# Decayed attention: projections and splits two heads earlier, q spread ahead of k, the division one score later

## The reference

```python
B, S, E, H = (2, 256, 128, 16)
D = E // H
b, s, e = x.shape
qkv = x @ Wqkv_w.T + Wqkv_b
qkv = qkv.reshape(b, s, 3, H, D).transpose(2, 0, 3, 1, 4)
q, k, v = (qkv[0], qkv[1], qkv[2])
scores = jnp.einsum('bhsd,bhtd->bhst', q, k) / jnp.sqrt(jnp.asarray(D, x.dtype))
dist = jnp.abs(idx[:, None] - idx[None, :])
decay = jnp.exp(-jnp.abs(distance_decay[0]) * dist)
scores = scores * decay
attn = jax.nn.softmax(scores, axis=-1)
out = jnp.einsum('bhst,bhtd->bhsd', attn, v)
out = out.transpose(0, 2, 1, 3).reshape(b, s, e)
return out @ out_w.T + out_b
```

## Time and profile before

| | |
|---|---|
| median of 3 runs | 2450.01 us (2449.64 to 2451.04) |
| the profiled execution | 2449.7 us, of which the traced span is 2447.9 us |
| busy share: PE, DVE, ACT, POOL | 90%, 67%, 61%, 69% |
| mean granted TensorE clock | 0.962 of full speed |
| phase `a` | some 1045 to 1701 us |

### The profile page before, as it was taken

The page is one execution under the profiler, slowest core; times in us unless marked ns, Lnnn a source line. Parts: engine busy times, 40 slices in busy tenths (PEclk is TensorE's granted clock), DMA queues, the critical chain, the costliest instruction groups (busy, mean ns, idle before and its releaser), DMA issues.

```text
span 2447.9 us, 60289 instructions
## 1 busy us (share of the span) xinstructions
PE 2202.7 (90%) x19744; PEld 1500.7 (61%) x19760; DVE 1628.1 (67%) x3905; ACT 1487.5 (61%) x4130; POOL 1679.2 (69%) x1712
## 2 busy tenths in 40 slices
PE   6998799998989998949998889998999979999989
PEld 4776467775657775525555555554677755677755
DVE  5777578875567775636665566666788755677755
ACT  3555378886378886325554455554788853788853
POOL 6777699884188884247665667665899831888842
PEclk8999899999999998979999999999999999999999
DMA  4000011121111111121101110110111211111111
GB/s 108 1 0 1 6 39 31 27 46 28 41 43 36 36 34 26 36 61 53 43 21 41 52 46 20 38 52 17 29 37 28 46 23 46 41 36 33 35 28 49
DMA packets 121250, 86.69 MB, mean 35 GB/s; under 512 B 85560, under 2 KB 102160, under 8 KB 118800
## 3 DMA queue, kind: packets, MB, share of 16 engines
q1 hardware_dynamic: 119248, 82.70, 14.1%
q10 hardware_dynamic: 1856, 2.23, 0.3%
HBM read 30.38 MB, written 8.39 MB: 16 GB/s over the span
## 4 chain that ended last, share of the span: by engine, by line
PE 50%; DVE 12%; POOL 9%; issue 8%; DMA 5%; SPq 3%; ACT 1%; DVEq 0%; POOLq 0%
PE bank L1170 8%; POOL store L1010 6%; PE bank L519 6%; PE bank L638 5%; PE bank L1161 4%; PE bank L1181 4%; DMA store<-parts 4%; PE bank L553 3%; PE bank L566 3%; PE bank L592 3%; PE bank L647 3%; PE bank L533 3%; DVE store L842 2%; POOL store L1019 2%; DVE store L847 2%
## 5 line engine op out<-in xcount | busy, mean ns | idle before, releaser
L1398 POOL TENSOR_SCALAR store<-store 128x512 f32<-128x512 f32 x512 | 349.8, 697 | 217.9 <-DVE store L1315 216.2
L1272 ACT ACTIVATE store<-bank 128x512 f32<-128x512 f32 x512 | 285.9, 604 | 316.4 <-PE bank L1170 315.6
L1315 DVE CUSTOM_DVE_ANT_0 store<-bank,store 128x512 f32<-128x512 f32 x512 | 340.2, 689 | 189.4 <-PE bank L1161 118.9
L730 ACT ACTIVATE store<-bank,store 128x128 f32<-128x128 f32 x1024 | 364.2, 378 | 68.6 <-DVE store L860 68.5
L1010 POOL TENSOR_TENSOR store<-store 128x16 f32<-128x16 f32 x128 | 372.6, 2911 | 26.4 <-DVE store L856 26.4
L1004 POOL TENSOR_TENSOR store<-store 128x512 f32<-128x512 f32 x256 | 321.2, 1276 | 83.3 <-DVE store L847 82.0
L1170 PEld LDWEIGHTS bank<-store 128*128 128x128 f32 x2048 | 252.4, 147 | 136.3 <-ACT store L1272 78.3
L1170 PE MATMUL bank<-store 128*128 128x128 f32 x2048 | 309.7, 285 | 0.0
L519 PE MATMUL bank<-store 128*128 128x512 f32 x512 | 268.8, 612 | 8.5 <-DVE store L835 7.0
L1019 POOL TENSOR_TENSOR store<-store 128x512 f32<-128x512 f32 x256 | 261.6, 1043 | 17.4 <-POOL store L1010 11.4
L1161 PE MATMUL bank<-store 72*128 72x512 bf16 x512 | 186.6, 397 | 86.1 <-DMA store<-parts 46.8
(11 more groups left out here) (199 smaller groups left out, 4457.7 us busy)
## 6 DMA issues: line engine op xcount, KB each, us to landing
store<-store SPq DMA_DIRECT2D x256, 128.0 KB, 2.3
store<-parts SPq DMA_DIRECT2D x96, 192.0 KB
parts<-store SPq DMA_DIRECT2D x16, 384.0 KB, 2.5
store<-store SPq DMA_DIRECT2D x128, 32.0 KB
store<-store SPq DMA_DIRECT2D x128, 31.8 KB
store<-store SPq DMA_DIRECT2D x32, 127.0 KB
store<-in_L_ffn_wqkv_dram SPq DMA_DIRECT2D x4, 768.0 KB, 4.5
out_dram<-store SPq DMA_DIRECT2D x8, 256.0 KB, 2.6
```

The costliest lines, as they stand in the source:

```text
L730: last = nc.scalar.activation(prob[:, e, b, :], bank[3 + e][:, b * P:(b + 1) * P], ACT.Exp, bias=nmax[:, e, b:b + 1], accum_out=psums[:, h ...
L1272: nc.scalar.activation(AT[:, h % 4, c, :], bank[2 + c][:, :], ACT.Exp, scale=-1.0).then_inc(aexp_done, 1)
L1315: nc.vector.tensor_tensor_reduce(out=S[:, h % 4, t, :], in0=bank[t % 2][:, :], in1=decay[:, off:off + L], scale=1.0, scalar=-3.0e38, op0=A ...
L1398: nc.gpsimd.tensor_scalar(s_, s_, -1.0, amax[:, h % 4, t:t + 1], ALU.mult, ALU.add).then_inc(shifted_done, 1)
```

## The change

Five edits, all in phase `a`:

- PE, ACT: transposing, projecting and biasing the next sequence stand after heads 2, 3 and 4 instead of 4, 5 and 6. `out_transpose` and `out_project` of the sequence before move from after heads 2, 3 to heads 5 and 6, with the copy on ACT. The waits that guard bank 7 move with them.
- POOL: three steps of q's split stand after head 6 and three of k's after head 8; before, two steps each after heads 8, 9 and 10. `stage` moves from head 3 to 1, `add_bias` from 1 to 3.
- SP: q is sent and its first half spread, then k sent and its first half spread. Before, both were sent first.
- DVE: `divide` and `take_values` move from behind the fourth score of heads 3, 7, 11, 15 to behind the first score of heads 4, 8, 12 and of head 0 of the next sequence.
- DVE: `add_out` stands after head 9 instead of 5, ahead of the statistics.

```diff
@@ -1097,34 +1097,38 @@
 
 
         def decayed_sp(sp):
-            def combine(q, half):
+            def combine(t, half):
 
                 heads = slice(half * HA // 2, (half + 1) * HA // 2)
-                for t, to in ((0, QC), (1, KC)):
-                    parts = parts_dram[t].rearrange("a (d h) n -> a d (h n)", d=DA)[:, :, half * HALF:(half + 1) * HALF]
-                    for x in range(PARTS):
-                        rows = to[x * PARTS * DA:(x + 1) * PARTS * DA, heads, :].rearrange("r h n -> r (h n)")
-                        sp.dma_start(rows, bc(parts[x], 0, PARTS) if t == 0 else parts).then_inc(combos_in[half], 16)
-
-            def send(q):
-                for t in range(2):
-                    sp.wait_ge(apart_ready, 2 * q + t + 1)
-                    sp.dma_start(parts_dram[t].rearrange("a p n -> p a n"), apart[:, t, :, :]).then_inc(parts_out, 16)
-                sp.wait_ge(parts_out, 32 * (q + 1))
-
-            send(0)
-            combine(0, 0)
-            combine(0, 1)
+                to = (QC, KC)[t]
+                parts = parts_dram[t].rearrange("a (d h) n -> a d (h n)", d=DA)[:, :, half * HALF:(half + 1) * HALF]
+                for x in range(PARTS):
+                    rows = to[x * PARTS * DA:(x + 1) * PARTS * DA, heads, :].rearrange("r h n -> r (h n)")
+                    sp.dma_start(rows, bc(parts[x], 0, PARTS) if t == 0 else parts).then_inc(combos_in[half], 16)
+
+            def send(q, t):
+                sp.wait_ge(apart_ready, 2 * q + t + 1)
+                sp.dma_start(parts_dram[t].rearrange("a p n -> p a n"), apart[:, t, :, :]).then_inc(parts_out, 16)
+                sp.wait_ge(parts_out, 32 * q + 16 * (t + 1))
+
+            for t in range(2):
+                send(0, t)
+                combine(t, 0)
+            for t in range(2):
+                combine(t, 1)
             load_ff(sp, 0)
             with sp.Fori(0, B - 1) as q:
 
                 for half in range(2):
                     sp.wait_ge(combos_in[half], (q + 1) * (16 * COMBOS))
-                send(q + 1)
-                sp.wait_ge(score_done, 64 * q + 32)
-                combine(q + 1, 0)
+                for t in range(2):
+                    send(q + 1, t)
+                    if t == 0:
+                        sp.wait_ge(score_done, 64 * q + 32)
+                    combine(t, 0)
                 sp.wait_ge(score_done, 64 * q + 64)
-                combine(q + 1, 1)
+                for t in range(2):
+                    combine(t, 1)
 
         def decayed_pe(pe):
             def x_transpose(q, first=False):
@@ -1188,9 +1192,12 @@
                     last = nc.tensor.transpose(bank[6][:, t * P:(t + 1) * P], aoT[:, t * P:(t + 1) * P], ident)
                 last.then_inc(ao_done, 1)
 
-            def out_transpose(q, more=True):
+            def out_transpose(q, more, ahead):
                 pe.wait_ge(ao_ready, 4 * q + 5)
-                pe.wait_ge(av_ready, q + 2 if more else q + 1)
+                if ahead:
+                    pe.wait_ge(afull_ready, 2 * q + 6)
+                else:
+                    pe.wait_ge(av_ready, q + 2 if more else q + 1)
                 for t in range(TPS):
                     last = nc.tensor.transpose(bank[7][:, t * P:(t + 1) * P], ao[:, t, :], ident)
                 last.then_inc(aobT_done, 1)
@@ -1225,19 +1232,16 @@
                             untranspose(q - 1, 3)
                         project_v(q)
                     elif h % 4 == 1:
+                        if before and h == 5:
+                            out_transpose(q - 1, True, more)
                         untranspose(q, h // 4 - 1)
-                    if before and h == 2:
-                        out_transpose(q - 1)
-                    if before and h == 3:
+                    if more and h == 2:
+                        pe.wait_ge(av_ready, q + 1)
+                        x_transpose(q + 1)
+                    if more and h in (3, 4):
+                        project(q + 1, h - 3)
+                    if before and h == 6:
                         out_project(q - 1)
-                    if more and h == 4:
-                        if before:
-                            pe.wait_ge(aout_added, q)
-                        else:
-                            pe.wait_ge(av_ready, q + 1)
-                        x_transpose(q + 1)
-                    if more and h in (5, 6):
-                        project(q + 1, h - 5)
 
             x_transpose(0, True)
             project(0, 0)
@@ -1251,7 +1255,7 @@
             for c in range(TPS):
                 weigh(B - 1, 3, c)
             untranspose(B - 1, 3)
-            out_transpose(B - 1, False)
+            out_transpose(B - 1, False, False)
             out_project(B - 1)
 
         def decayed_act(act):
@@ -1286,14 +1290,14 @@
                         copy_oT(q - 1, 3)
                     elif h % 4 == 0 and h:
                         copy_oT(q, h // 4 - 1)
-                    if h == 2 and before:
+                    if more and h == 2:
+                        copy_xT(q + 1)
+                    if more and h in (3, 4):
+                        if h == 3:
+                            act.wait_ge(parts_out, q * 32 + 32)
+                        with_bias(q + 1, h - 3)
+                    if h == 5 and before:
                         copy_out(q - 1)
-                    if more and h == 4:
-                        copy_xT(q + 1)
-                    if more and h in (5, 6):
-                        if h == 5:
-                            act.wait_ge(parts_out, q * 32 + 32)
-                        with_bias(q + 1, h - 5)
 
             copy_xT(0)
             with_bias(0, 0)
@@ -1339,13 +1343,13 @@
                 for h in range(HA):
                     for t in range(TPS):
                         scale_scores(q, h, t)
-                    if h == 3:
-                        if before:
-                            divide(q - 1, 3)
-                        take_values(q)
-                    elif h % 4 == 3:
-                        divide(q, h // 4 - 1)
-                    if h == 5 and before:
+                        if t == 0 and h < 8 and h % 4 == 0 and before:
+                            divide(q - 1, 2 + h // 4)
+                        if t == 0 and h >= 8 and h % 4 == 0:
+                            divide(q, h // 4 - 2)
+                        if t == 0 and h == 4:
+                            take_values(q)
+                    if h == 9 and before:
                         add_out(q - 1)
                     if norm_more and h == 9:
                         norm_stats(dve, LN_START + LN_STEPS * NORM_A + 2 + q, q + 2, FIRST)
@@ -1363,6 +1367,7 @@
                 sequence(q, True, True, True)
             sequence(B - 2, True, True)
             sequence(B - 1, True, False, False, True)
+            divide(B - 1, 2)
             divide(B - 1, 3)
             add_out(B - 1)
 
@@ -1401,17 +1406,17 @@
                 for h in range(HA):
                     for t in range(TPS):
                         subtract_max(q, h, t)
-                    if h == 1:
+                    if h == 3:
                         add_bias(q)
                     if norm_more and h == 10:
                         norm_rstd(pool, LN_START + LN_STEPS * NORM_A + 2 + q, FIRST)
                     if norm_next and h == 10:
                         norm_rstd(pool, LN_START + LN_STEPS * NORM[1] + 1, 0, FIRST)
-                    if more and h == 3:
+                    if more and h == 1:
                         stage(q + 1)
-                    if more and h in (8, 9, 10):
-                        for i in (2 * h - 16, 2 * h - 15):
-                            split(q + 1, i // 3, i % 3)
+                    if more and h in (6, 8):
+                        for step in range(3):
+                            split(q + 1, h // 2 - 3, step)
 
             for t in range(2):
                 for step in range(3):
```

## The result

The changed kernel takes 2385.91 us (median of 4 runs, 2384.87 to 2388.03) against 2450.53 us of the kernel before beside it: a ratio of 0.9731, 95% interval 0.971 to 0.9751. The forecast was 2394, its range 2382 to 2413. The profiled execution took 2385.01 us with a span of 2383.2, which is 64.7 us less than before. The phase `a`, measured from its first `x_transpose` to the start of its last `out_project`, went from 654.3 to 588.2 us. So the whole difference, 66.1 us, lies there, and 1.4 us were lost elsewhere.

A forecast was written before the change was run, and what follows sets the result against it. PE's own instructions were taken as the floor, its waits and half-clock stretches as the possible gain. Gains of 26.7 + 12.5 + 14.4 - 3.6 + 6 = 56.0 us off 2449.7 gave 2394 us, range 2382 to 2413.

The forecast's parts named there:

- (A): DVE's loop jump keeps its price, PE's wait after it staying near 5 us with half clock: 2408 us, chance 0.14.
- (B): DVE's jump costs PE nothing and the clock stays at 2.4 GHz, all 45.1 us gained: 2376 us, chance 0.08.
- (C): PE's waits after the divisions don't vanish, the 0.2 us of slack being eaten: 2408 us, chance 0.10.
- (D): k's parts come late at sequence boundaries, a longer wait at score 64: 2470 us, chance 0.04.
- (E): PE's waits were not for copies but something moving with them: within 0.2% of 2450 us, chance 0.04.
- four looped windows: Head 12 to next sequence's head 0, passes where DVE jumps back: each still loses 4.6 us, 26.7 us gained.
- three unrolled windows: The same head 12 to head 0 stretches in unrolled code: lose some 0.3 us in all, 12.5 us gained.
- Step 1: Sequence boundaries: projections, splits and copies come earlier, fourteen us of slack, so all seven DMA waits go.
- Step 2: Pass end on DVE: with division moved, a 3.4 us jump runs beside PE's work, leaving a 2.9 us wait.
- Step 3: Heads 2 and 10: with division one score on, PE's waits after untransposes go, 14.4 us gained.
- Step 4: DVE after score 39: output adding directly ahead of the statistics makes PE wait, 3.6 us lost.
- Step 5: Phase start: q spread before k's send, k's send queued behind it, first score earlier, 6 us gained.

The follow-up runs named there:

- e1: The changed kernel with DVE's divisions and the taking of v back behind the fourth score of heads 3, 7, 11, 15: 2438.65 us.
- e7: The kernel before with the second half's copies held back until ten scores of the next sequence are done: 2443.39 us.
- e9: The changed kernel with the division in its old place and the second half's copies held back ten scores: 2431.63 us.
- e3: The kernel before with only the divisions and the taking of v moved one score later: 2414.76 us.
- e5: The kernel before with DVE's loop over sequences 1 to 5 written out, so DVE never jumps back: 2423.77 us.
- e6: The changed kernel with the adding of the output after DVE's head 10 instead of head 9: 2385.19 us.
- e2: The changed kernel with SP's old order, both parts sent before q and k are spread: 2392.12 us.

## Why the prediction was right

The mechanism held, and each rival fell by a row: PE's waits behind the jump are 1.56 to 1.75 us and not near 5 (A), but none of the four is zero, and the clock fell once (B), heads 2 and 10 show no wait (C), no copy is waited for in a boundary (D), and the time is not that of before (E). The forecast is 8 us too high: the phase gained 10.1 us more than the sum, 1.4 us were lost elsewhere, and the median lies 0.9 us above the profiled execution. Term by term, in us gained in the phase:

| step | predicted | measured |
|---|---|---|
| four looped windows | 26.7 | 36.0 (45.1 - 9.2) |
| three unrolled windows | 12.5 | 12.8 |
| waits in heads 2, 10 less the added work (all between the windows) | 14.4 - 3.6 = 10.8 | 11.6 |
| start | 6 | 5.7 (32.8 to 27.1 from first transpose to first score) |
| sum | 56.0 | 66.1 |

The looped windows are the term that was off. Their 36.0 us lie above the 17 to 32 that the prediction gave as bounds, and two of its signs did not come: these windows last 17.7 to 19.5 us and not near 20.5, and the idle time behind DVE's last scaling is 2.56 to 2.75 us and not 3 to 4. The total stayed in its range because the other three terms were within 1 us of theirs.

**Step 1, the copies earlier**, was right: all seven DMA waits are gone. POOL's three splits stand in a row at 1175.44 to 1178.62, and no score waits for POOL. SP issued k's spread at 1183.39, 20 us ahead of score 64 at 1203.38. But the prediction booked the DMA waits as a gain of their own, and e1 shows that they are not: in a window the saved 3 us are partly eaten by a longer jump, which then lies in the traffic. Only both edits together bring the sum.

**Step 2, the mis-sized term.** A looped window was to lose 2.9 + 1.6 + 0.1 = 4.6 us; three lost 1.8 to 2.0 and one 3.6. Three sizes were off, all in one direction. The jump took 2.60, 2.56, 2.75 and 2.75 us and not 3.4: the four rows of before had all been taken behind a division and with copies running at 74 to 95 GB/s, and even the lowest, 3.07, was too high for one ahead of the copies. DVE also finished its last scaling 1.27 us after score 63 began (1202.71 to 1203.98), not 1.57, because the scaling before it starts 0.57 us after its score and not 0.93. The later start stands in the looped sequences of every kernel with the division at the end of the pass (before, e1, e7, e9: idle 1.04 to 1.05 us ahead of it), and not in e3, nor in e5, which has that division but no jump (0.69 to 0.71). Why is open. That makes a wait of 1.76 us for 2.9. And the half clock, which stood behind both single waits of about 3 us in the kernel before, followed one of the four waits here:

```profile
1417.85 0.39 PE L1165 MATMUL bank<-store 72*128 72x512 bf16 x1 [1.75 <-DVE store L1319]
1418.08 1.71 PE L1174 MATMUL bank<-store 128*128 128x128 f32 x8
1419.58 0.63 PE L1165 MATMUL bank<-store 72*128 72x512 bf16 x1
```

The wait of 1.75 us in the window before (at 1347.62) has no such stretch behind it. Rival A's "against", that the jump begins before that traffic, was the right reading, and e1 with e9 show it; the forecast should have drawn the jump's length from it too.

**Step 3** was right: no wait remains in heads 2 and 10, with the slack of 0.2 us. (The list of waits has one in head 2 too few: the trace has eight and not seven, 0.9 us more.) In e1, with the division in its old place, waits of 0.73 and 0.77 us stand in heads 2 and 10 again. So they belong to the division's place.

**Step 4** was right in kind and 1.1 us too dear: the new waits ahead of head 8's third weighing are 0.22 us as printed, 0.38 in real time, not 0.57, and the last sequence lost 0.6:

```profile
1599.44 0.39 PE L1165 MATMUL bank<-store 72*128 72x512 bf16 x1 [0.90 <-DVE store L1319]
1600.05 0.39 PE L1165 MATMUL bank<-store 72*128 72x512 bf16 x1 [0.22 <-DVE store L1319]
```

**Step 5** was right, queueing and all: k's spread was issued at 1066.20 (predicted "near 1065"), the first score started at 1071.93 (predicted near 1071). The rule of the Trainium skill named there, in "DMA: Bandwidth & Descriptors", section "Why a DMA increments its semaphore by 16 and not by 1", agrees with this trace: between 1061 and 1065 the DMA share is 0.19, three engines of sixteen, and k's send of 2.66 us took 9.1 behind the spread of three copies.

## What to carry to other kernels

A loop's jump back stalls its engine for some microseconds; put the last thing that others wait for well ahead of it, and nothing that itself waits for them just before it, so that the stall runs beside work or beside a wait that is there anyway. Two waits in a row that come from one dependency are not two terms of a sum: ask which of them would hide the other if the order changed, and test the edits singly. Before a stall's length is taken from the trace, look at what the DMA did beside those rows, and whether it will do the same where the stall is to stand.

## What the runs showed of the hardware

- The jump back of DVE's loop took 2.92 to 3.13 us behind a division with almost no copies running (3 GB/s), 3.07 to 5.01 us in the kernel before, and 4.70 to 5.23 us beside copies of 132 to 138 GB/s. Behind a scaling, with the copies just starting (50 to 66 GB/s on the mean), it took 2.56 to 2.75 us. One packet of 8 KB on a DMA queue of kind "instruction" falls into each jump. It starts 0.4 to 0.6 us after DVE's last instruction in the changed kernel, 0.8 in e7 and e9, 0.8 to 2.5 in the kernel before and 2.0 to 2.5 in e1, and DVE resumes 1.7 to 2.2 us after its end. That puts the 0.3 us between the changed kernel and e9 ahead of the packet; why it starts earlier behind a scaling was not tested.
- The fall of TensorE's clock to 1.2 GHz behind a wait is not decided by that wait's length alone. After waits of 1.60, 1.56 and 1.75 us it stayed at 2.4 GHz, after another of 1.75 us it fell. In e6 it fell after one of 1.76 us, in e2 it stayed after one of 1.81. In e3 waits of 1.97, 2.47, 2.78, 2.95 and 3.33 us left it up and waits of 2.43 and 3.14 us did not. In e5, windows with waits of 2.76 to 3.31 us all had a mean of 0.92, one with 2.66 us had 1.00. What decides it stays open; a fall cost 1.6 to 1.7 us in the changed kernel and in e3.
- A send of 384 KB behind the spread of q took 9.1 us to land and not 2.7, though q's spread alone occupies only a fifth of the DMA engines' time (0.19, at 79 GB/s, from 1061 to 1065 in the changed kernel).
